# Two-layer expert kernel: the weighting and adding of gathered rows moved to GpSimd, and the row buffers, fills and order of steps around it

## What is computed

```python
x = x + 0.5 * ffn(layernorm(x), gate_w, w1, w3, w2)
x = x + attn(layernorm(x), ...)        # an RWKV mix: k, v, r projections, a scan over time
x = x + 0.5 * ffn(layernorm(x), gate_w, w1, w3, w2)
```

```python
h   = silu(x @ w1[i]) * (x @ w3[i])    # 128 -> 512
out = out + (h @ w2[i]) * w_i          # 512 -> 128
```

## Time and profile before

| | us |
|---|---|
| median of 3 runs | 611.98 (611.75 to 612.49) |
| the profiled execution, its own time | 611.98 |
| its span, first to last instruction | 610.1 |
| PE busy / DVE busy / POOL busy / ACT busy | 517.9 / 423.6 / 389.0 / 318.7 |
| mean granted TensorE clock | 0.98 of full speed |

### The profile page before, as it was taken

The page is one execution under the profiler, slowest core; times in us unless marked ns, Lnnn a source line. Parts: engine busy times, 40 slices in busy tenths (PEclk is TensorE's granted clock), DMA queues, the critical chain, the costliest instruction groups (busy, mean ns, idle before and its releaser), DMA issues.

```text
span 610.1 us, 18551 instructions
## 1 busy us (share of the span) xinstructions
PE 517.9 (85%) x5866; PEld 474.2 (78%) x5866; DVE 423.6 (69%) x1218; ACT 318.7 (52%) x703; POOL 389.0 (64%) x490
## 2 busy tenths in 40 slices
PE   1234899999999899998999989999999999999930
PEld 1233789898988789877898779898788899998930
DVE  4861963556878998889999895887788766225431
ACT  5432664444584666666585654676465454444410
POOL 1171049499999990399935999102957998955973
PEclk9999999999999999999999999999999999999985
DMA  8963233555232222212321133111121442323332
GB/s 280 328 209 110 69 92 110 145 148 127 83 105 79 67 80 57 71 62 70 83 71 46 58 113 92 45 51 32 53 84 54 122 111 88 102 62 105 85 91 60
DMA packets 89062, 59.55 MB, mean 98 GB/s; under 512 B 10256, under 2 KB 82704, under 8 KB 88976
## 3 DMA queue, kind: packets, MB, share of 16 engines
q1 hardware_dynamic: 55296, 29.97, 16.9%
q0 software_dynamic: 8192, 16.79, 9.0%
q10 hardware_dynamic: 25488, 11.61, 6.7%
HBM read 28.65 MB, written 29.69 MB: 96 GB/s over the span
## 4 chain that ended last, share of the span: by engine, by line
PE 55%; DVE 14%; ACT 12%; POOL 8%; issue 7%; DMA 3%; POOLq 0%; ACTq 0%; DVEq 0%; SPq 0%
PE py L1260 17%; PE pa L1246 14%; PE pb L1246 12%; POOL rows_in L726 3%; ACT xn L818 3%; DVE h L1115 3%; POOL yg L738 3%; PE bkB L1319 2%; PE pT L1233 2%; PE bkB L1298 2%; ACT sil L799 2%; POOL pace L755 2%; PE bkA L1313 2%; DVE stats L905 2%; PE bkA L1298 1%
## 5 line engine op out<-in xcount | busy, mean ns | idle before, releaser
L726 POOL DMA_INDIRECT rows_in<-parts,slot x128 | 134.9, 1054 | 175.7 <-DVE slot L1040 153.8
L1260 PE MATMUL py<-ffn_w,h 128*128 x1416 | 196.2, 282 | 9.4 <-ACT yrow L784 9.0
L1115 DVE TENSOR_TENSOR h<-sil,pb 128x512 f32<-128x512 f32 x177 | 120.7, 686 | 116.8 <-ACT sil L799 76.6
L1260 PEld LDWEIGHTS py<-ffn_w,h 128*128 128x128 f32 x1416 | 172.6, 192 | 15.5 <-issue 12.3
L1246 PE MATMUL pa<-rT,ffn_w 128*128 128x128 f16 (+1 forms) x1752 | 150.3, 232 | 14.9 <-DVE h L1115 11.8
L1246 PE MATMUL pb<-rT,ffn_w 128*128 128x128 f16 (+1 forms) x1752 | 154.4, 232 | 0.0
L738 POOL DMA_INDIRECT yg<-rows_out,slot x128 | 125.1, 978 | 35.0 <-issue 22.8
L1246 PEld LDWEIGHTS pa<-rT,ffn_w 128*128 x1752 | 123.3, 99 | 29.5 <-issue 18.4
L755 POOL MEMSET pace<- 128x544 uint8 x223 | 127.6, 572 | 0.2
L1246 PEld LDWEIGHTS pb<-rT,ffn_w 128*128 x1752 | 121.8, 98 | 6.9
L799 ACT ACTIVATE sil<-pa 128x512 f32<-128x512 f32 x177 | 105.4, 595 | 31.8 <-PE pa L1246 31.7
(11 more groups left out here) (156 smaller groups left out, 458.8 us busy)
## 6 DMA issues: line engine op xcount, KB each, us to landing
rows_out<-yrow ACTq DMA_DIRECT2D x177, 64.0 KB, 1.9
rin<-rows_in SPq DMA_DIRECT2D x65, 128.0 KB
rows_in<-zrow SPq DMA_DIRECT2D x34, 128.0 KB, 2.1
shared<-in_w SPq DMA_DIRECT2D x16, 256.0 KB, 6.7
rin<-rows_in SPq DMA_DIRECT2D x47, 64.0 KB
rows_in<-zrow SPq DMA_DIRECT2D x2, 1472.0 KB, 11.2
xres<-in_x SPq DMA_DIRECT2D x4, 512.0 KB, 6.5
ffn_w<-in_w SPq DMA_DIRECT2D x8, 256.0 KB, 4.7
```

Of the source, the lines that this page charges most:

```text
L726: pool.indirect_dma_start(rows_in[g][:], bass.IndirectOffsetOnAxis(ap=slot[:, c, at:at + 1], axis=0), parts[:, at, :], None).then_inc(s_sc ...
L1115: dve.tensor_tensor(h[:, t % RING, :], sil[:, t % 2, :], pb[t % 2][:], ALU.mult).then_inc(s_h, 1)
L1260: mm = pe.matmul(py[:], h[:, step % RING, at:at + T], w, start=(c == 0), stop=(c == FC - 1))
```

## The change

1. **GpSimd sums.** For each block of 128 tokens whose two gathers have landed, POOL multiplies each of the two rows by its weight (`scale`, two `tensor_scalar`) and adds them (`add_up`, one `tensor_tensor`); these stand between later transfers, and a pace memset is issued only between two transfers that follow each other directly. DVE's combine becomes one 128x512 add, behind `s_summed`. Units of the last pass are combined as before.
2. **Gathered when done.** The first run of a pass with two is gathered when its own rows are done (`GEND`: tile 115 in place of 131 for run 4, tile 154 in place of 162 for run 6, each plus 3).
3. **Buffers and fills.** Each of the seven passes has its own `rows_in` and `rows_out`. Only the first is filled by one DMA ahead of the tiles; the others are filled in pieces of 256 rows in SP's loop, the second pass's 12 pieces at tiles 0 to 11.
4. **Order.** CHOOSE of run 1 moves ahead of tile 0; the two `norm` of run 1 move ahead of the weight splits 3 to 7; `DUE_SHIFT` and `NOT_BEFORE` are empty; the planner's costs and its model of POOL are new.

```diff
-WORK = {"dve": {"combine": 2.6, "stats": 1.3, ...
+WORK = {"dve": {"combine": 0.75, "stats": 1.3, ...
-SPACE = 1.6
-DUE_SHIFT = {
...
-NOT_BEFORE = {
...
+TRANSFER, SPACED, SCALED, SUMMED, ARRIVE, OWN = 1.13, 0.59, 0.6, 0.47, 2.3, 0.75
+BEHIND = 2
+DUE_SHIFT = {}
+NOT_BEFORE = {}
-PEND = tuple(sum(PASS_STEPS[:PASS[r] + 1]) for r in range(RUNS))
+HEAD_STEPS = tuple((units[0] * S * TOPK + E * (T - 1)) // T for units in PASSES)
+GEND = tuple(PSTART[r] + (HEAD_STEPS if OPEN[r] else PASS_STEPS)[PASS[r]] for r in range(RUNS))
-    soon(1, *(("stats", b) for b in one), ("rsqrt", 0))
+    soon(1, *(("stats", b) for b in one), ("rsqrt", 0), *(("norm", b) for b in one))
     soon(0, *(("split", e) for e in range(3, E)))
-    soon(1, *((step, b) for b in one for step in ("norm", "turn", "xnT", "hi", "lo", "logits", "keep")))
+    soon(1, *((step, b) for b in one for step in ("turn", "xnT", "logits", "hi", "keep")), *(("lo", b) for b in one))
+    soon(1, *((step, 0) for step in CHOOSE))
```

In the planner's model of POOL:

```diff
-            free["pool"] = max(free["pool"], asked) + SPACE
+            free["pool"] = max(free["pool"], asked) + TRANSFER
             transfers.append((tile, name, run, *many.pop(0)))
+            moved[0] += 1
+            if name == "gather" and transfers[-1][5] == TOPK - 1:
+                fetched.append(["scale", *transfers[-1][2:5], free["pool"] + ARRIVE, moved[0]])
+            if fetched and moved[0] >= fetched[0][5] + BEHIND:
+                finish_block(tile, True)
+            else:
+                free["pool"] += SPACED
```

On POOL:

```diff
+            def scale(run, b, j):
+                n, at = GATHERS.index((run, b)), (U0[run] + b) * JU + j
+                pool.wait_ge(s_wts, run + 1)
+                pool.wait_ge(s_gat[n % GSLOTS][j], 16 * TOPK * (n // GSLOTS + 1))
+                for c in range(TOPK):
+                    y = yg[:, n % GSLOTS, c, j, :]
+                    pool.tensor_scalar(y, y, wts[:, c, at:at + 1], None, ALU.mult).then_inc(s_scaled, 1)
+            def add_up(run, b, j):
+                n = GATHERS.index((run, b))
+                pool.wait_ge(s_scaled, TOPK * (n * JU + j + 1))
+                pool.tensor_tensor(yg[:, n % GSLOTS, 0, j, :], yg[:, n % GSLOTS, 0, j, :], yg[:, n % GSLOTS, 1, j, :],
+                                   ALU.add).then_inc(s_summed, 1)
...
+                follows = TRANSFERS[i + 1][1] if i + 1 < len(TRANSFERS) else None
+                if name in MOVES and follows in MOVES and t < TILES - 1:
+                    wait(pool, s_pace, spaced - PACES + 1)
+                    pool.memset(pace[:, spaced % PACES, :], 0).then_inc(s_pace, 1)
+                    spaced += 1
```

On DVE, in `combine`:

```diff
-                dve.wait_ge(s_gat[n % GSLOTS], 16 * TOPK * JU * (n // GSLOTS + 1))
-                for c in range(TOPK):
+                if GEND[run] < TILES:
+                    dve.wait_ge(s_summed, JU * (n + 1))
+                    ins = dve.tensor_tensor(xres[:, js, :], xres[:, js, :], yg[:, n % GSLOTS, 0, :, :], ALU.add)
```

More of the change, by code:

```diff
@@ L80 @@
 SKEW = 3
-FILLED_FIRST = 2
 FILL = 256
@@ L232, in make_plan @@
     never = 1e9
-    route(1, [])
     for run in range(2, R1):
@@ L245, in make_plan @@
     for run in range(R1, RUNS):
-        for b in range(UNITS[run] if PEND[run] < TILES else 0):
+        for b in range(UNITS[run] if GEND[run] < TILES else 0):
             gathered[run, b] = chain(FINISH, run, b, (START[min(run + 2, RUNS - 1)], 3), never)
@@ L329, in ask @@
         waiting.append([due, at, name, run, [(b, j, c) for b in units for j in range(JU) for c in range(TOPK)]])
+    ask(0.0, START[1] - 3, "scatter", 1, range(UNITS[1]))
     def in_use(run, unit):
@@ L335, in in_use, with finish_block @@
         return n >= GSLOTS and "combine" not in gathered[order[n - GSLOTS]].ends
+    def finish_block(tile, spaced):
+        step, run, b, j, landed, _ = fetched[0]
+        start = max(free["pool"], landed if step == "scale" else 0.0)
+        free["pool"] = start + (SCALED if step == "scale" else SUMMED + OWN * (not spaced))
+        transfers.append((tile, step, run, b, j, 0))
+        if step == "scale":
+            fetched[0][0] = "sum"
+            return
+        fetched.pop(0)
+        if j == JU - 1:
+            gathered[run, b].start = free["pool"]
     def send(tile, until):
@@ L341, in send @@
             at = max([free["pool"]] + [min((w[1] for w in now), default=until)])
+            while fetched and (not now or at > free["pool"] + OWN) and max(free["pool"], fetched[0][4]) < until:
+                finish_block(tile, False)
+            at = max(at, free["pool"])
             if not now or at >= until:
@@ L377, in make_plan @@
         for run in range(RUNS):
-            if tile == PEND[run] + SKEW:
+            if tile == GEND[run] + SKEW:
                 for b in range(UNITS[run]):
@@ L395, in make_plan @@
             assert found or len(transfers) > sent
-    last = [(TILES, step, run, b) for run in range(RUNS) if PEND[run] == TILES
+    last = [(TILES, step, run, b) for run in range(RUNS) if GEND[run] == TILES
             for step in ("gather", "combine", "write") for b in range(UNITS[run])]
@@ L407, in count @@
     return order.index(upto) + 1
+MOVES = ("scatter", "gather")
 GATHERS = [p[2:] for p in PLAN if p[1] == "gather"]
@@ L657, in _ @@
                 load_x(g)
-            for piece in fills[1]:
-                fill(piece, s_fill)
-            later = [(piece, s_fill) for g in range(2, SETS) for piece in fills[g]]
-            later += [(piece, s_rest) for g in range(SETS) for piece in rests[g]]
+            for piece in rests[0]:
+                fill(piece, s_rest)
+            later = [(piece, filled) for g in range(1, len(PASSES)) for many, filled in ((fills, s_fill), (rests, s_rest))
+                     for piece in many[g]]
             def load(q):
@@ L747, in _ @@
                 scatter(*one)
-            for sent, (t, name, *one) in enumerate(TRANSFERS):
-                if name == "scatter":
-                    scatter(*one)
-                else:
-                    gather(*one)
-                if t < TILES - 1:
-                    wait(pool, s_pace, sent - PACES + 1)
-                    pool.memset(pace[:, sent % PACES, :], 0).then_inc(s_pace, 1)
+            def scale(run, b, j):
[10 more added lines that the diff above has]
+                                   ALU.add).then_inc(s_summed, 1)
+            spaced = 0
+            for i, (t, name, run, b, j, c) in enumerate(TRANSFERS):
+                if name == "scatter":
+                    scatter(run, b, j, c)
+                if name == "gather":
+                    gather(run, b, j, c)
+                if name == "scale":
+                    scale(run, b, j)
+                if name == "sum":
+                    add_up(run, b, j)
+                follows = TRANSFERS[i + 1][1] if i + 1 < len(TRANSFERS) else None
[3 more added lines that the diff above has]
+                    spaced += 1
             for run in range(RUNS):
-                for one in every(run, range(UNITS[run] if PEND[run] == TILES else 0)):
+                for one in every(run, range(UNITS[run] if GEND[run] == TILES else 0)):
                     gather(*one)
```

64 lines of the change are left out of this document (31 added, 33 removed), and 6 rows, old and new, of the table NOT_BEFORE.

## The result

The changed kernel takes 691.14 us (median of 4 runs, 690.25 to 691.47) beside 612.00 for the kernel before on the same chip: ratio 1.129, 95% interval 1.127 to 1.131, so 79 us slower. The forecast was 608.3 (598 to 619) with 0.59 on faster: wrong in sign and far outside its range.

The account below looks back on a forecast made before the run. PE was taken as the bound, idle only 25.3 us between tiles. From 611.98, +1.1 (b), -2.6 (a, b, c), 0 (d, e, g) and -1.8 (f) gave 608.7; some tenths less, 608.3 was predicted, range 598 to 619.

Parts of the forecast that it names:

- the limit on the gain (25 us): PE between the tiles: its idle time sums to 25.3 us, so relieving another engine returns no more than about 25.
- Part a: DVE's combine: one 0.68 us add replaces 2.33 us in 15 units, taking 24.8 us of DVE work away.
- DVE busy about 30 us lower: Sign that the forecast is right: DVE's total busy time falls by about 30 us.
- Part b: CHOOSE of run 1 ahead of tile 0: 8.8 us of DVE work moves into idle time; start costs +1.1 us.
- Part d: POOL's time for a block: 3.4 us before, 3.3 after, taken as equal; nothing booked.
- Rival 3: DVE waits at combine for POOL's sum, delaying h and PE: 12 us less 4.4 of gains, 620; chance 0.17.
- Part e: Zero fills in pieces: run 1's first scatter moves to about 87.6, later fills precede their scatters; booked 0, bound +2.
- Part f: Early gathers of first groups in the second layer: pays at the end alone, -1.8 us, bounds -2.1 and 0.
- Part g: Order without the 40 hand corrections, planner with new costs: booked 0, gain bounded at 25 us, loss at +12.6.
- Part c: Port locks between DVE and POOL: 5 us of DVE work comes back, bounds 0 and 14.

Follow-up runs that it names:

- e7: e4 without the two scales, so POOL adds the two rows unweighted: 613.27 us, ratio 1.002.
- e15: Kernel before with only CHOOSE of run 1 and its norms moved ahead of tile 0: 612.44 us, ratio 1.002.
- e4: Kernel before with the GpSimd scales and sums alone, order and fills kept: 646.54 us, ratio 1.056.
- e6: Kernel before with only the second pass's fill cut into 12 pieces, the third pass's moved behind it: 619.61 us, ratio 1.013.
- e1: Changed kernel with the second pass filled by one DMA ahead of the tiles again: 657.10 us, ratio 1.073.
- e2: e1 with later fill pieces of 768 rows in place of 256: 645.72 us, ratio 1.054.
- e8: Kernel before with only the early gathers, a pass's first run gathered when its own tiles are stored: 622.07 us, ratio 1.016.
- e20: Kernel before with early gathers for run 6 alone: 611.17 us, ratio 0.9983.
- e5: Kernel before with only DUE_SHIFT and NOT_BEFORE emptied: 615.84 us, ratio 1.006.
- e9: e2 with the sums back on DVE: 628.49 us, ratio 1.027.
- e3: Changed kernel with the sums back on DVE, fills as changed: 665.32 us, ratio 1.086.
- e13: e4 with the scales taking a constant in place of the weight: 637.99 us, ratio 1.0435.
- e10: e2 with the planner's costs of POOL set to what the trace shows: 644.76 us, ratio 1.055.

## Why the prediction was wrong

- **What bounds the kernel.** Right for before; no run came near the limit on the gain (25 us). What I did not ask is how much slack POOL has: between 83 and 224 us its transfers and memsets follow each other with a single pause, of 7.8 us. A view of POOL's timeline instead of its 64% share would have shown it.
- **Part a, combine:** the add takes 0.692 us (0.68 taken), and the combines' busy time falls from 34.1 to 10.4 us, 23.7 for the 24.8 booked. Right. What it returns was hidden by the other parts; the nearest is e7, 3.5 us at the last tile. "DVE busy about 30 us lower" was wrong as a sign, since CHOOSE's 8.8 us only move and stay in DVE's total.
- **Part b, CHOOSE early:** right step by step up to tile 2. ACT kept the last logits at 47.10 (47.2), CHOOSE's last row came at 56.10 (56.0), the first silu at 59.95 (59.9), and the first h ended at 61.32 (61.2). Tile 2 began on PE at 61.56, +1.5 where +1.1 was booked. But tile 3 then waited 3.75 us for h, and the low clock followed; in e15, with the tables of before, the same change costs 0.6 us in all. The rows of after:

```profile
47.10 0.20 ACT L877 ACTIVATE logit<-bkB 128x32 f32<-128x32 f32 x1 [1.51 <-PE bkB L1361]
...
56.10 0.17 DVE L1116 TENSOR_SCALAR wts<-ed 128x8 f32<-128x8 f32 x1
...
60.63 0.69 DVE L1152 TENSOR_TENSOR h<-sil,pb 128x512 f32<-128x512 f32 x1 [2.85 <-ACT sil L836]
...
66.79 1.44 PE L1288 MATMUL pa<-rT,ffn_w 128*128 128x256 f16 x6 [3.75 <-DVE h L1152]
```

- **Part d, POOL's own time: the step that failed first.** "After: two transfers 2.26, two scales 0.6, the sum 0.45, in sum 3.3. Equal; I book nothing." The block is 4.01 us. The wrong term is the scale, priced by the plain copy at 0.289 and so at 0.3; it takes 0.645. Sixty blocks x (4.01 - 3.39) = 37 us on POOL, and e4 lost 34. With the memset's 0.572 as the upper bound for a scale, a block is 3.85 us and sixty are 27 us over; I never set that out, and never set the total against POOL's free time where gathers run.
- **Rival 3** named the right wait in the right place, and put 12 x 0.5 x 2 us on it. DVE waited 59.9 us for POOL in e4 and 79.5 in the kernel after; the price of 620 is 27 us short of e4, and the chance of 0.17 was too low. The figure counted only the stretched locks and the delay of one block; it left out, as e4 against e7 shows, that POOL falls further behind with each block of a batch, because a block is longer than what it replaced.
- **Part e, fills: the larger failure.** "I book 0, bound +2". The count for run 1 holds: alone, its scatters start at 89.2 for 87.6, and tile 23 is 1.2 late (e6). In the kernel after they start at 97.67, since tile 10 itself was made 8.8 us later. The sentence "The fills of later passes, tiles 12 to 79, come before the scatters that need them" is wrong: they come one for each tile, so that 12 pieces ahead of them are 12 tiles' delay. e6 prices that at 7.3 us, e1 and e2 at 34 and 45 with the order of the kernel after. I had looked at the first scatter and not at what stands behind a waiting scatter in POOL's queue, which is the first gather.
- **Part f, first groups gathered when done:** booked -1.8, "nobody but the output waits for a gather". The mechanism at the end is there: in the kernel after the last eight gathers begin 2.64 us behind the last store's issue (669.73 - 667.09), where it was 4.12, and in e8 the end is 2.1 shorter. But nothing waits for a gather while everything behind it in POOL's queue does: run 4's gathers hold run 7's scatters by 16 us. The step failed for run 4 and held for run 6 (e20).
- **Part g, the order:** booked 0. The emptied tables alone cost +3.6 (e5), inside its bounds; the whole order, with the planner's new costs, was never run alone.
- **Part c, locks:** booked 5 us of DVE work that comes back, bounds 0 and 14. DVE's busy time beside the combine grew by 7 us in e4 and by 2 in e7, which keep the order of before, and by 9 in the kernel after; e4 and e7 differ by the scales, 5 us. So the size is right, though e9, without sums on POOL, has 5 us more too, and no run shows that it is the lock. On POOL's side the slowest scale of the kernel after takes 1.51 us where 0.61 is usual; it starts at 519.93, while DVE runs two 128x512 instructions with both inputs in SBUF (from 519.70 and 520.30, 0.69 us each). The Trainium skill, SBUF — State Buffer (the two separate sides), says that of such a pair of instructions the one that starts first holds the shared ports and the other is blocked; this trace agrees in direction.

The Trainium skill's advice in GPSIMD Engine Reference, on elementwise work, to keep such work on VectorE was right here: e3 and e9 gained 26 and 17 us by it.

## What to carry to other kernels

An engine that issues the DMAs in order is a queue: whatever is put on it, or ahead in it, delays all behind it, and a step's cost is its own time plus what stands behind it until the next pause. Price an operation by a row of the same kind, or take the dearest near row; a plain copy is no price for a scale, and a term that is 0.3 us too small, taken 120 times on an engine without slack, cost 34 us here. Where two late things meet in one queue, the parts done alone can add to less (here 56 us) than the whole (79).

## What the runs showed of the hardware that was not expected

- On POOL, one `tensor_scalar` of 128x128 fp32 takes 0.566 us with a constant (e13) and 0.633 to 0.666 with a weight per partition (e4, e10), more than a `tensor_tensor` of two inputs of the same size (0.494 to 0.509) and twice the one plain copy.
- Stalls of PE cost a second time: 16.4 us of longer matmuls beside 63.7 us of more idle time. While PE idled from 175 to 211 us the granted clock stood at 0.50, and it was at 1.00 again from 217; the estimate by windows puts 15 of the 16.4 us on such rows.
- A gather directly behind two scales takes 1.01 us, one behind a memset 0.96 (medians of 44 and 31 in the kernel after); over all 128 the mean went from 978 to 1030 ns. Why wasn't tested. The group in the kernel after:

```profile
L755 POOL DMA_INDIRECT yg<-rows_out,slot x128 | 131.8, 1030 | 62.0 <-issue 53.1
```
